# Value projection before the products, query projections in a row, and one masked sum per head on VectorE in the first attention of a two-layer vision transformer

## The reference, cut to what matters

```python
q, k, v = split(layernorm(h) @ Wqkv + bqkv)                 # 8 heads of 64
scores = einsum('bhnd,bhmd->bhnm', q, k) * SCALE            # 65 x 65 for each image and head
top_val = top_k(scores, 64)[..., -1:]                       # the 64th largest of 65
scores = where(scores < top_val, -inf, scores)
attn = softmax(scores)
v_curr, res = v, 0
for i in range(3):
    v_curr = attn @ v_curr
    res += gelu(alphas_raw[i]) * v_curr
h = h + res @ Wout + bout
```

## Time and profile before

| | |
|---|---|
| median of 3 runs | 1797.75 us (1796.31 to 1799.28) |
| the profiled execution, its own time | 1796.46 us |
| its span, first to last instruction | 1794.6 us |
| mean granted TensorE clock | 0.970 of full |
| busy over the whole span: PE, DVE, ACT, POOL | 92%, 60%, 47%, 43% |

### The profile page before, as it was taken

One profiled execution on the slowest core, in us unless ns is written; L12 is line 12 of the kernel. 1 busy time (PEld: TensorE's weight loads), 2 busy tenths in 40 slices (PEclk: granted clock), 3 DMA queues, 4 the chain that ended last, 5 costly groups with the idle time before them and its releaser, 6 DMA issues. The chain is left out here.

```text
span 1794.6 us, 61648 instructions
## 1 busy us (share of the span) xinstructions
PE 1654.6 (92%) x24187; PEld 1223.5 (68%) x24187; DVE 1083.3 (60%) x3361; ACT 849.9 (47%) x2334; POOL 778.0 (43%) x932
## 2 busy tenths in 40 slices
PE   8999998899999999987899989999999999779997
PEld 3444444677777777764777747777777777569897
DVE  0000006887888888883666654667676767757764
ACT  0000005665655656652444455666666666356653
POOL 0000000877888788881011113345554545534444
PEclk9999999999999999998699999999999999789999
DMA  9887740000000000003000000000000000134422
GB/s 362 342 324 301 281 169 1 3 4 3 3 3 4 3 3 3 3 4 102 4 1 1 1 4 3 3 14 24 17 23 17 23 17 23 40 105 128 119 67 59
DMA packets 47213, 117.16 MB, mean 65 GB/s; under 512 B 10731, under 2 KB 29470, under 8 KB 46972
## 3 DMA queue, kind: packets, MB, share of 16 engines
q1 hardware_dynamic: 39198, 99.25, 15.3%
q0 software_dynamic: 6096, 12.94, 2.1%
q10 hardware_dynamic: 1678, 1.43, 0.3%
HBM read 96.80 MB, written 18.61 MB: 64 GB/s over the span
## 5 line engine op out<-in xcount | busy, mean ns | idle before, releaser
L1457 PE MATMUL ps<-xn,s_a_wqkv 128*128 128x260 f32 x1024 | 300.6, 411 | 29.5 <-ACT qk_a L856 23.2
L201 PE MATMUL ps<-x_chunk,s_w_tok 128*128 128x512 f32 x576 | 251.6, 598 | 6.5 <-DMA x_chunk<-in_x_main 6.5
L1457 PEld LDWEIGHTS ps<-xn,s_a_wqkv 128*128 128x128 f32 x1024 | 170.2, 191 | 104.8 <-ACT qk_a L856 70.0
L201 PEld LDWEIGHTS ps<-x_chunk,s_w_tok 128*128 128x128 f32 x576 | 109.8, 192 | 147.0 <-issue 147.0
L1032 ACT ACTIVATE e_a<-e_a 128x585 f32<-128x585 f32 (+1 forms) x128 | 84.9, 663 | 170.4 <-DVE e_a L1343 98.3
L813 POOL TENSOR_TENSOR prob_a<-e_a,inv_sum_a 128x512 f32<-128x512 f32 x64 | 67.1, 1048 | 225.7 <-issue 125.4
L228 DVE SCALAR_TENSOR_TENSOR h<-ps,s_b_tok,s_pos 128x512 f32 (+1 forms) x16 | 11.3, 746 | 248.3 <-PE ps L209 248.3
L1541 PE MATMUL ps<-s_a_wqkv,xn_pair_a 128*64 128x256 f32 x1024 | 139.4, 392 | 4.5 <-ACT weightsT_m L963 2.8
L1334 DVE TENSOR_REDUCE neg_max_a<-ps 128x8 f32<-128x520 f32 x128 | 89.2, 697 | 89.1 <-PE ps L1435 89.1
L2106 POOL DMA_INDIRECT out<-h,xn x93 | 92.9, 999 | 114.0 <-DVE h L2219 107.4
L797 POOL TENSOR_TENSOR kept_a<-e_a,keep_a 128x585 f32<-128x585 f32 x64 | 87.2, 1363 | 89.7 <-issue 79.0
(11 more groups left out here) (278 smaller groups left out, 4336.4 us busy)
## 6 DMA issues: line engine op xcount, KB each, us to landing
x_chunk<-in_x_main SPq DMA_DIRECT2D x96, 768.0 KB, 8.8
xn<-pair_rows SPq DMA_DIRECT2D x93, 130.0 KB, 2.1
pair_rows<-pad_rows_m SPq DMA_DIRECT2D x29, 130.0 KB
s_f_all<-in_f_w SPq DMA_DIRECT2D x2, 1024.0 KB
x_ends<-in_x_tail SPq DMA_DIRECT2D x16, 96.0 KB, 10.7
out<-h,xn POOLq DMA_INDIRECT x93
s_w_tok<-in_w_tok SPq DMA_DIRECT2D x6, 192.0 KB, 8.2
pair_rows<-rows_m,slot_i_m POOLq DMA_INDIRECT x65, 2.5
```

The source lines that it names most:

```text
L201: last = nc.tensor.matmul(ps[:, bank, :], w_tok[:, k, :], xb[:, s, k, :], start=(k == 0), stop=False)
L1457: nc.tensor.matmul(ps[:, QK_BANK[i], 0:QUAD], w_qkv[:, c * P:(c + 1) * P], xn[:, t.h * QUAD:(t.h + 1) * QUAD], start=True, stop=True).then ...
```

## The change

The change is in the first attention alone (the other branch gets the same conditions in other places of the text). It does this:

- The order of PE's step becomes `scores`, `project_v`, `products`, `transpose_cls`, `project_qk` four times, `transpose_probs`, `project_out`. The banks become 6, 4, 5, 7 for the four query or key chunks, 2 for the transposed probabilities, 7 for the values and for the class column, and the waits follow from that: `transpose_probs` now waits for `c_done[0]` of its own step.
- DVE's comparison for all heads (L1358, L1361), POOL's multiplication (L797) and DVE's sum (L1375) are replaced by one scalar_tensor_tensor per head on DVE, eight in a step and a ninth in even steps: (scores <= bound) * e, written to `kept`, with the sum of the row as a second output (`accum_out`) to `total`. The tile `keep` is gone.
- ACT copies the values first in its step, takes the four query or key chunks in a row, and scales the values from their copy in SBUF (`v_raw`) in place of PSUM.

```diff
             low8 = sb(f"low8_{tag}", [P, 2, CH + 1, 8])
-            keep = sb(f"keep_{tag}", [P, 2, CH + 1, SEQ])
             kept = sb(f"kept_{tag}", [P, 2, CH + 1, SEQ])
...
         if masked:
-            low_done, keep_done, kept_done = s("low_done"), s("keep_done"), s("kept_done")
+            low_done, kept_done = s("low_done"), s("kept_done")
             va_done, dsum_done = s("va_done"), s("dsum_done")
...
 
-        QK_BANK, R_BANK, T_BANK, V_BANK, C_BANK = (((6, 7, 6, 7), (4, 5), 5, 4, 5) if masked else
+        QK_BANK, R_BANK, T_BANK, V_BANK, C_BANK = (((6, 4, 5, 7), (4, 5), 2, 7, 7) if masked else
                                                    ((4, 5, 4, 5), (2, 3), 3, 6, 2))
...
                                             ALU.mult).then_inc(va_done, 1)
-                if masked and t.has(2):
-                    upto(pool, exp_done, t.s - 1, pairs)
-                    upto(pool, keep_done, t.s - 1, pairs)
-                    upto(pool, norm_done, t.s - 2, pairs)
-                    nc.gpsimd.tensor_tensor(columns(kept, t.even), columns(e_of(t), t.even),
-                                            columns(keep, t.even), ALU.mult).then_inc(kept_done, 1)
                 if masked and t.has(3):
...
                     return
-                src = ps[:, V_BANK, :].rearrange("p (i c d) -> p i c d", i=2, c=CH)
+                upto(act, v_sb, t.s - 1, pairs)
                 upto(act, dsum_done, t.s - 5, pairs)
                 for c in range(CH):
-                    last = nc.scalar.activation(dv[:, (t.j - 2) % 4, :, c, :], src[:, :, c, :], ACT.Copy,
+                    last = nc.scalar.activation(dv[:, (t.j - 2) % 4, :, c, :], v_raw[:, t.j % 2, :, c, :], ACT.Copy,
                                                 scale=alphas[:, c, 2:3])
...
                 if masked:
+                    values_out(t)
                     exps(t)
...
                     product_out(t, 1)
-                    qk_out(t, 0)
                     cls_probs_out(t)
-                    qk_out(t, 1)
-                    values_out(t)
+                    for i in range(4):
+                        qk_out(t, i)
                 else:
...
                     dist_out(t)
-                qk_out(t, 2)
-                qk_out(t, 3)
+                    qk_out(t, 2)
+                    qk_out(t, 3)
                 scaled_values_out(t)
...
                     upto(dve, low_done, t.s - 1, pairs)
-                    last = nc.vector.tensor_tensor(keep[:, :, 0:CH], score(), over_keys(low8[:, :, 0:CH, 1]),
-                                                   ALU.is_le)
+                    upto(dve, exp_done, t.s - 1, pairs)
+                    upto(dve, norm_done, t.s - 2, pairs)
+                    for b in range(2):
+                        for c in range(CH):
+                            last = nc.vector.scalar_tensor_tensor(
+                                out=kept[:, b, c, :], in0=score()[:, b, c, :], scalar=low8[:, b, c, 1:2],
+                                in1=e_of(t)[:, b, c, :], op0=ALU.is_le, op1=ALU.mult,
+                                accum_out=total[:, b, c:c + 1])
                     if t.even:
-                        last = nc.vector.tensor_scalar(keep[:, 0, CH], cls_score(), low8[:, 0, CH, 1:2],
-                                                       None, ALU.is_le)
-                    last.then_inc(keep_done, 1)
+                        last = nc.vector.scalar_tensor_tensor(
+                            out=kept[:, 0, CH, :], in0=cls_score(), scalar=low8[:, 0, CH, 1:2],
+                            in1=e_of(t)[:, 0, CH, :], op0=ALU.is_le, op1=ALU.mult,
+                            accum_out=total[:, 0, CH:CH + 1])
+                    last.then_inc(kept_done, 1)
                 order_out(t, 0)
...
                         sums, invs = total[:, :, 0:CH], inv[:, :, 0:CH]
-                    nc.vector.tensor_reduce(sums, columns(kept_of(t), t.even), AX.X, ALU.add).then_inc(sum_done, 1)
-                    upto(dve, sum_done, t.s - 1, pairs)
+                    if not masked:
+                        nc.vector.tensor_reduce(sums, columns(kept_of(t), t.even), AX.X, ALU.add).then_inc(sum_done, 1)
+                        upto(dve, sum_done, t.s - 1, pairs)
                     upto(dve, norm_done, t.s - 2, pairs)
...
                     upto(pe, cq_done, t.h, quads)
-                upto(pe, keep_done if masked else below_done, t.s - 2, pairs)
+                upto(pe, kept_done if masked else below_done, t.s - 2, pairs)
                 sl, first = (t.j - 2) // 2 % 2, 0 if t.even else 2
...
                 if masked:
-                    if i == 0 and t.even:
-                        upto(pe, qk_sb, 4 * t.s - 1, 4 * pairs)
-                    elif i == 0:
-                        upto(pe, qk_sb, 4 * t.s - 1, 4 * pairs)
-                        upto(pe, o_added, t.h - 3, quads)
-                    elif i == 1:
+                    if i == 0:
                         upto(pe, qk_sb, 4 * t.s, 4 * pairs)
+                        if not t.even:
+                            upto(pe, o_added, t.h - 3, quads)
+                    elif i < 3:
+                        upto(pe, r_sb, 2 * (t.s - lag_r) + i, images)
                     else:
-                        upto(pe, qk_sb, 4 * t.s + i - 1, 4 * pairs)
+                        upto(pe, v_sb, t.s - 1, pairs)
+                        if not t.even:
+                            upto(pe, tc_sb, t.h, quads)
                 else:
...
 
+                upto(pe, qk_sb, 4 * t.s, 4 * pairs)
                 upto(pe, dv_done, t.s - 2, pairs)
...
                 upto(pe, xs_copied, t.s - 1, pairs)
+                upto(pe, v_sb, t.s - 2, pairs)
                 if masked:
-                    upto(pe, r_sb, 2 * (t.s - lag_r) + 1, images)
-                    if t.edge:
-                        upto(pe, dv_done, t.s - 2, pairs)
+                    upto(pe, qk_sb, 4 * t.s, 4 * pairs)
+                    upto(pe, tc_sb, t.h - 1, quads)
                 else:
-                    upto(pe, v_sb, t.s - 2, pairs)
                     if route:
...
                 upto(pe, norm_done, t.s - 2, pairs)
-                upto(pe, r_sb, 2 * (t.s - lag_r) + (2 if masked else 1), images)
-                if masked and t.edge:
-                    upto(pe, t_sb, t.s - 3, pairs)
+                if masked:
+                    upto(pe, v_sb, t.s - 1, pairs)
+                else:
+                    upto(pe, r_sb, 2 * (t.s - lag_r) + 1, images)
                 pick = ident[:, :].rearrange("p (i x) -> p i x", i=4)[:, :, 0:H]\
...
                 upto(pe, norm_done, t.s - 2, pairs)
-                upto(pe, r_sb, 2 * (t.s - lag_r) + 2, images)
-                if masked and t.edge:
-                    upto(pe, t_sb, t.s - 3, pairs)
-                if masked and not t.even:
-                    upto(pe, tc_sb, t.h, quads)
+                if masked:
+                    upto(pe, c_done[0], t.s - 3, pairs)
+                    if t.edge:
+                        upto(pe, t_sb, t.s - 3, pairs)
+                else:
+                    upto(pe, r_sb, 2 * (t.s - lag_r) + 2, images)
                 chunks = prob[:, (t.j - 3) % 2].rearrange("p h k -> p (h k)")
...
                     upto(pe, r_sb, 2 * t.s - 12, images)
-                    upto(pe, qk_sb, 4 * t.s + 3, 4 * pairs)
+                    upto(pe, qk_sb, 4 * t.s + 1, 4 * pairs)
                 else:
...
                 if masked:
+                    project_v(t)
                     products(t)
-                    project_qk(t, 0)
-                    project_qk(t, 1)
                     transpose_cls(t)
-                    project_v(t)
-                    project_qk(t, 2)
-                    project_qk(t, 3)
+                    for i in range(4):
+                        project_qk(t, i)
                     transpose_probs(t)
```

## The result

| | before | after |
|---|---|---|
| median | 1797.35 us (14 runs) | 1804.93 us (14 runs) |
| the profiled execution, its own time | 1796.46 us | 1803.32 us |
| its span | 1794.6 us | 1801.5 us |

The ratio is 1.0050, with a 95% interval of 1.0036 to 1.0065: some 9 us slower (the two medians differ by 7.6 us), where 28 us were forecast (29 us above the profiled execution). The time lies in the range, the direction is right, the size is off by a factor of three.

The account below looks back on a forecast made before the run. PE was taken to bound the kernel. A new wait of 47 us less 18 us of hidden stalls leaves 29 us on the profiled 1796.46, given as a median of 1826 us; range 1800 to 1862.

Parts of the forecast that it names:

- What bounds the kernel: First attention: PE, busy 95%, sets the pace; making it wait for an engine is enough to lose time.
- The new wait, the main term: PE's transposes wait for DVE's addition behind the masked sums: 1.17 us in even, 0.31 in odd steps, 47 us in all.
- the price of one masked sum: On DVE, the pitch of one masked sum with its second output: 0.19 + 0.07 = 0.26 us.
- The hand-over from DVE to PE: Between DVE's addition and PE's transposes: allowed 0.07 us.
- PE's new order, costed at little: PE's values ahead of products, four query chunks together: same work elsewhere, 0.1 to 0.2 us uncovered that cost nothing.
- the stalls: PE's stalls without a releaser, about 20 us in the stage: 18 taken as hidden by the new wait.
- POOL's part and ACT's copies: POOL's 1.44 us multiplication goes away, ACT copies the values from SBUF: both costed at nothing.
- (a): Rival on DVE: a cheap masked sum of 0.19 us, second output free, about 1807 us; chance 0.18.
- (b): Rival on DVE: a dear masked sum of 0.35 us, 1875 us; chance 0.14 with what lies between.
- (c): Rival: not slower, possibly faster; masked sums at a 0.13 us pitch, separate banks fill PE's holes, 1791 us; chance 0.11.
- (d): Rival: PE's stalls all go as its queue fills while waiting, 20 us hidden, not 18; no chance of its own.

Follow-up runs that it names:

- e1_add_first: The changed kernel with DVE's first addition, which frees bank 2, moved from behind the masked sums to in front of them: 1786.19 us, ratio 0.9939 to before.
- e3_old_mask: The changed kernel with the old masking and DVE's old sum, keeping the change's PE order, banks and waits: 1781.47 us, ratio 0.9918 to before.
- e5_no_accum: The changed kernel without the second output (accum_out) of the masked products, DVE summing them in one instruction as before: ratio 1.0034 to before.
- e6_values_behind: e3_old_mask with the values projected behind the products instead of in front of them: ratio 1.0050 to the kernel before.

## Why the prediction was right or wrong

- **What bounds the kernel: right.** PE did set the pace, and to lose it was enough to make it wait.
- **The new wait, the main term: right in kind, too large.** Its place and releaser are as forecast, it comes back in most even steps (23 waits in the 28 of the 450 us), and e1_add_first, where it is gone, takes it back. The step that failed is the price of one masked sum: 0.26 us, measured 0.207. I added 0.07 us, the pitch of a tiny instruction, for the accumulator; it costs 0.013, since it is read while the next operation starts. The hand-over from DVE to PE was too small: 0.15 us (DVE's addition starts at 559.82 and lasts 0.68, the transposes start at 560.65), not 0.07. With both, the even step is 4.34 + 1.86 + 0.68 + 0.15 = 7.03 us, which is what was measured. In the odd step DVE begins masking 3.33 us behind PE's start (550.48 - 547.15, 0.1 earlier than before); 3.33 + 8 x 0.207 + 0.83 = 5.82 us, just when PE gets there. So the odd step has no wait in place of 0.31 us, and 1.48 us for two steps became 0.79 (0.84 with 0.05 by which the shortest odd step is longer, also where nothing waits, as in e3_old_mask).
- **A small term that was missing.** Every second even step is longer by 0.2 us (9.56, from 537.59 to 547.15). In it DVE is idle for 0.24 us in front of an operation that waits for its own predecessor; in the other even steps it is 0.04. It comes once in four steps, and DVE's instructions are a loop over four steps, so I take it for the loop's new round; no run tests that. Before the change the same place has 0.13 us, and PE did not wait for it:

```profile
540.02 0.70 DVE L1336 TENSOR_TENSOR e_a<-ps,neg_max_a 128x520 f32<-128x520 f32 x1 [0.24 <-DVE neg_max_a L1329]
```

- **PE's new order, costed at little: wrong.** I took it for the same work elsewhere. It takes away 0.52 us for two steps (15.88 to 15.36 in e3_old_mask), a ratio of 0.9918 by itself. The prediction did have the stalls shrink, by 18 of 20 us, but credited it to the wait. On top of the new order the wait takes away less: from 0.33 us above the shortest steps in e3_old_mask to 0.12 in the change (0.22 less the 0.1 of the loop). No run has the wait with the old order, so how much it would have hidden there is not known. That the rows before put 17.8 us to "issue" should have raised the question what the order does to them. There was also more to take away than I counted: 0.90 us above the shortest steps is 29 us for 32 pairs of steps, not 20, and the 15.11 us that I took for two steps without a stall is 14.98.
- **Where the error of the sum lies.** In steps, the change costs 0.16 x 32 = 5 us, 24 us less than the forecast's 29. Of these, 20 are the wait (47 forecast, 0.84 x 32 = 27 measured) and 7 the stalls (18 forecast, 0.78 x 32 = 25 measured); the loop gives back 3.
- **The sum by measured parts.** The order: 0.9918. The masked sums on top of it, with the wait they cause: 1.0050 / 0.9918 = 1.0133, 24 us. The masked sums without the shared bank: 0.9997. So neither part is slow by itself; the loss is their meeting at bank 2.
- **POOL's part and ACT's copies: right at nothing.** ACT's four scaled copies from SBUF take 1.26 us (1.13 before), within the slack.
- **Rivals.** (a) had nearly the right pitch, 0.19, and gave 1807; the measured 1804.9 is nearest to it. That its time fits so well is luck in part: its 17 us of wait were 27, and its 8 us of hidden stalls were 25. I gave it 0.18 and the forecast 0.57, for an argument on the accumulator for which there was no row. (b) and (c) did not happen. (d) happened in part, and mostly for another reason.

## What to carry to other kernels

When two purposes come to share a PSUM bank, follow the new wait through the order of the engine that releases it: here one addition stood behind nine instructions that it did not need, and putting it first (e1_add_first) turned a loss of 0.5% into a gain of 0.6%. An engine's idle time without a releaser is not a constant of the kernel; here it depended on the order of long and short instructions, and it should be costed as a term of a reordering. Look in the transfers too: code is loaded as well as data. And take a change apart before judging it: one half of this one was worth 0.8%, the other nothing where no bank ties it to PE, and together they lost.

## What the runs showed of the hardware

- The read of an accumulator on DVE takes 0.08 us, starts at the same time as the next operation, and adds 0.013 to 0.014 us to the pitch (median 0.192 without it in e5_no_accum, 0.206 with it in the change).
- With eight long matmuls between two rows of short ones PE stalls without a releaser for 9 us in 450 (e3_old_mask), with the same matmuls behind the second row for 20 us (e6_values_behind).
- These stalls end 2.1 to 3.0 us after the start of a 16 KB transfer of instructions in 163 of 170 cases; such a transfer takes about 1.0 us.
- DVE is idle for 0.24 us once in four steps where it waits for its own predecessor (13 times in 450 us of the change), 0.13 us at the same place before.
